# A two-layer MetaFormer kernel on one core: the pipeline one group deeper, the weight broadcast in pieces, the expert sums on VectorE

## The reference

```python
x = x + L0_conv(ln_c(x))      # projection, a linear state per image (KV = B^T V dA, y = C KV + D V), layer norm, W_out
t = t + L0_ffn(ln_t(t))       # mixture of 8 experts, hidden 128, top 2 of a softmax; weights w
x = x + L1_conv(ln_c(x))      # divisive normalisation: x * rsqrt(8x8 channel mix of x^2 + 3x3 depthwise of x^2 + beta)
t = t + L1_ffn(ln_t(t))       # mixture of 8 experts, hidden 256, top 2 of the logits
```

## Time and profile before

| | |
|---|---|
| median of 3 runs (745.37 to 746.63) | 746.52 us |
| the profiled execution's own time | 745.84 us |
| its span in the trace | 744.1 us |
| busy: PE, DVE, ACT, POOL | 566.3, 437.4, 372.7, 245.7 us |
| mean granted TensorE clock | 0.917 of full |

### The profile page before, as it was taken

How to read it: one execution, slowest core, us unless ns; L and a number is a source line. 1 busy time by engine, 2 the same in 40 slices (tenths; PEclk the granted TensorE clock), 3 DMA queues, 4 the chain that set the end, 5 groups by cost and what they waited for, 6 DMA issues and landing times.

```text
span 744.1 us, 10005 instructions
## 1 busy us (share of the span) xinstructions
PE 566.3 (76%) x3778; PEld 276.6 (37%) x3778; DVE 437.4 (59%) x810; ACT 372.7 (50%) x454; POOL 245.7 (33%) x217
## 2 busy tenths in 40 slices
PE   2645675579868995999768986998589968976677
PEld 1242253325423442445224532454244523432333
DVE  3255347454777569574967487756865495546412
ACT  2214322565446655575548554764557564644432
POOL 2020243122523344342442342434434243423103
PEclk9999875799989999899989998999899997989688
DMA  4501400515014500641052401450055005320140
GB/s 66 101 0 43 87 0 0 109 35 104 1 32 98 116 0 15 130 90 27 15 112 52 83 14 49 82 116 1 17 114 114 3 15 115 85 46 0 25 91 28
DMA packets 27838, 41.47 MB, mean 56 GB/s; under 512 B 11792, under 2 KB 19088, under 8 KB 27792
## 3 DMA queue, kind: packets, MB, share of 16 engines
q1 hardware_dynamic: 27152, 38.75, 25.4%
q0 software_dynamic: 640, 2.10, 0.9%
HBM read 38.22 MB, written 2.62 MB: 55 GB/s over the span
## 4 chain that ended last, share of the span: by engine, by line
PE 40%; DVE 27%; ACT 11%; DMA 8%; issue 7%; POOL 6%; SPq 1%; POOLq 0%; DVEq 0%; ACTq 0%
PE yP L863 11%; PE hP L847 11%; DMA WB<-w_scratch 6%; DVE nacc L1149 4%; PE sA L773 3%; PE sA L786 3%; PE sA L780 2%; PE sC L876 2%; ACT H L690 2%; ACT L574 2%; POOL stat_b L494 2%; DVE xsplit L979 2%; DVE xnrm L976 2%; DVE xcen_b L976 2%; PE sA L759 2%
## 5 line engine op out<-in xcount | busy, mean ns | idle before, releaser
L690 ACT ACTIVATE H<-hP,b 128x1024 f32<-128x1024 f32 x192 | 211.0, 1113 | 111.1 <-PE hP L847 108.4
L863 PE MATMUL yP<-H,w 128*64 128x512 f32 x768 | 208.9, 626 | 21.9 <-DVE ACC L1193 14.3
L847 PE MATMUL hP<-xT,w 128*64 128x512 f16 x1536 | 215.7, 406 | 10.6 <-ACT H L690 10.5
L552 POOL TENSOR_TENSOR ACC<-ACC,YW 128x512 f32<-128x512 f32 x96 | 125.4, 1310 | 212.6 <-DVE YW L1193 212.5
L847 PEld LDWEIGHTS hP<-xT,w 128*64 128x64 f16 x1536 | 83.2, 115 | 139.0 <-issue 74.1
L1193 DVE SCALAR_TENSOR_TENSOR YW<-yP,b,WB 128x512 f32<-128x512 f32 x96 | 71.4, 744 | 30.2 <-PE yP L863 30.1
L863 PEld LDWEIGHTS yP<-H,w 128*64 128x64 f32 x768 | 54.1, 143 | 61.7 <-issue 30.6
L1149 DVE SCALAR_TENSOR_TENSOR nacc<-PAD,taps,nacc 128x528 f32<-128x528 f32 x56 | 52.7, 941 | 1.7
L1193 DVE SCALAR_TENSOR_TENSOR ACC<-yP,b,WB 128x512 f32<-128x512 f32 x32 | 23.1, 745 | 41.7 <-DMA WB<-w_scratch 41.7
L1207 DVE TENSOR_TENSOR X<-sC,X 128x256 f32<-128x256 f32 x32 | 13.5, 423 | 53.9 <-PE sC L876 53.9
L876 PEld LDWEIGHTS sC<-fold,ACC 128*128 128x128 f32 x256 | 32.4, 198 | 25.6 <-issue 19.1
(11 more groups left out here) (144 smaller groups left out, 728.4 us busy)
## 6 DMA issues: line engine op xcount, KB each, us to landing
WB<-w_scratch SPq DMA_DIRECT2D x32, 1024.0 KB, 10.1
X<-in_x SPq DMA_DIRECT2D x8, 256.0 KB, 12.0
out<-X POOLq DMA_DIRECT2D x8, 256.0 KB, 2.8
H<-in_L_ffn_W SPq DMA_DIRECT2D x2, 512.0 KB, 6.7
H<-in_L_ffn_W SPq DMA_DIRECT2D x2, 256.0 KB, 4.2
w<-in_L_ffn_W SPq DMA_DIRECT2D x1, 512.0 KB, 5.2
w_scratch<-wTs SPq DMA_DIRECT2D x16, 32.0 KB, 1.8
w<-in_L_ffn_W SPq DMA_DIRECT2D x1, 256.0 KB, 4.4
```

The costliest lines, as they stand in the source:

```text
L552: pool.tensor_tensor(ACC[l][:, cols], ACC[l][:, cols], YW[:, u % 4, :], ALU.add).then_inc(summed, 1)
L690: nc.scalar.activation(H[:, s % RING, :], hP[s % 2][:, :], ACT.Gelu, bias=b1[l][:, e * ch + c:e * ch + c + 1], scale=1.0 / WS)\
L847: mm = nc.tensor.matmul(hP[s % 2][b * C:(b + 1) * C, hf * HALF:(hf + 1) * HALF], w1[l][:, sp, w, b * C:(b + 1) * C], xT[l][g % 2][:, hf * ...
L863: mm = nc.tensor.matmul(yP[hf][a * C:(a + 1) * C, :], w2[l][:, (2 * j + a) * ch + c, :], H[:, (2 * ch * j + 2 * c + a) % RING, hf * HALF:( ...
```

## The change

Four things change.

- **Depth.** A constant DEPTH = 2 enters `moe_start`: moe(0, g) starts at 24(g-2), moe(1, g) stays at 24g+8 as long as a group is still two ahead, and the last two, moe(1, 6) and moe(1, 7), follow each other without a gap (at 144 and 160). A section now holds moe(0, g+2), moe(1, g), most of ab(g+3), and cd(g+1). One section more (moe(0, 1) with ab(2) and cd(0), no moe(1, .)) stands ahead of the first full one, and one full one less follows. X3 gets a third buffer, and ACC is assigned by a table (moe(1, 6) uses the layer-0 accumulator).
- **Places.** cd(g) starts at moe_start(0, g)+16, and its steps are spread: in a section, the nine taps stand on slots 23, 0, 1 and 2 instead of 19 to 21, turn_u on 5 and 6 instead of 0, norm d on 10 instead of 4, its gate on 14 to 17 instead of 6 to 9. The table of ab is the same.
- **Pieces.** WB is filled by four pieces (an expert pair each, two DMAs of 256 KB), each with a semaphore of its own. A piece waits only until that pair of the group before is used. In layer 1 the pieces stand on slots 18, 22, 2 and 6.
- **Sums.** The adds to ACC are made by VectorE right behind the unit, waiting for it; GpSimd makes none.

```diff
 def moe_start(layer, g):
-    return SLOTS * (g - 1) if layer == 0 else SLOTS * g + E
+    if layer == 0:
+        return SLOTS * (g - DEPTH)
+    if g + DEPTH < GROUPS:
+        return SLOTS * g + E
+    return moe_start(1, g - 1) + E * CHUNKS[1]
...
 def cd_start(g):
-    return moe_start(0, g) + E * CHUNKS[0] + LAG + 2
+    return moe_start(0, g) + E * CHUNKS[0] + LAG + 4
...
-    cd=dict(centre_c=1, sums_c=1, norm_c=3, pool0=5, pool1=6, pool2=7, pool3=7, turn_u=10, centre_d=10,
-            sums_d=12, norm_d=14, top2=17, weights=18),
+    cd=dict(centre_c=0, sums_c=1, norm_c=3, pool0=7, pool1=8, pool2=9, pool3=10, turn_u=14, centre_d=15,
+            sums_d=16, norm_d=18, top2=23, weights=24),
...
+            def spread_piece(l, g, j):
                 if g >= 1:
-                    sp.wait_ge(scaled, 8 * (POS[(l, g - 1)] + 1))
+                    sp.wait_ge(scaled, 8 * POS[(l, g - 1)] + 2 * j + 2)
                 for a in range(2):
-                    src = scratch[l][i].rearrange("(j a) n -> a j n", a=2)[a]
-                    sp.dma_start(WB[l][a * C:a * C + C, :, :], src.partition_broadcast(C)).then_inc(w_in[l][i], 16)
+                    sp.dma_start(WB[l][a * C:a * C + C, j, :],
+                                 scratch[l][g % 2][2 * j + a:2 * j + a + 1, :].partition_broadcast(C)
+                                 .rearrange("c a n -> c (a n)")).then_inc(w_in[l][j], 16)
...
-                    pool.tensor_tensor(ACC[l][:, cols], ACC[l][:, cols], YW[:, u % 4, :], ALU.add).then_inc(summed, 1)
...
                     v.scalar_tensor_tensor(out=dst, in0=yP[hf][:, :], scalar=b2[l][:, j:j + 1],
                                            in1=WB[l][:, j, cols], op0=ALU.add, op1=ALU.mult).then_inc(scaled, 1)
+                    if j >= 1:
+                        acc = ACC[ACC_OF[m]][:, cols]
+                        dve.wait_ge(scaled, u + 1)
+                        v.tensor_tensor(acc, acc, dst, ALU.add).then_inc(summed, 1)
```

More of the change, by code:

```diff
@@ L54 @@
 LAG = 4
+DEPTH = 2
 NO_FINAL = (-1, -1, -1, -1)
@@ L58 @@
             mix_out=29, turn_b=32, gate=35, send=36),
-    cd=dict(turn_c=4, pool0=4, turn_u=11, turn_d=15, gate=16, send=19),
-    final=(12, 14, 24, 26))
+    cd=dict(turn_c=5, pool0=6, turn_u=13, turn_d=20, gate=22, send=25),
+    final=(13, 16, 24, 26))
 ACT_AT = dict(
@@ L77 @@
     ab=dict(decay=22, send=35),
-    cd=dict(send=21),
+    cd=dict(send=26, piece1=30, piece2=34, piece3=38),
     final=NO_FINAL)
@@ L136, in build_metaformer @@
         n += E * CHUNKS[m[0]]
+    ACC_OF = {m: 0 if m[0] == 0 or GROUPS - m[1] in range(2, DEPTH + 1) else 1 for m in ORDER}
+    ACC_BEFORE = {}
+    for i in range(2):
+        users = [m for m in ORDER if ACC_OF[m] == i]
+        ACC_BEFORE.update(zip(users[1:], users))
     with ExitStack() as ctx:
@@ L193, in build_metaformer @@
         X2b = sb("X2b", [P, T, C])
-        X3 = [sb(f"X3_{i}", [P, T, C]) for i in range(2)]
+        X3 = [sb(f"X3_{i}", [P, T, C]) for i in range(3)]
         X4 = [sb(f"X4_{i}", [P, T, C]) for i in range(2)]
@@ L281, in build_metaformer @@
         w_out = [[sem(f"w_out{l}_{i}") for i in range(2)] for l in range(2)]
-        w_in = [[sem(f"w_in{l}_{i}") for i in range(2)] for l in range(2)]
+        w_in = [[sem(f"w_in{l}_{j}") for j in range(PAIRS)] for l in range(2)]
         x2b = count("x2b", 1)
@@ L457, in ab @@
                     spread_weights(0, g)
+                    for j in range(PAIRS):
+                        spread_piece(0, g, j)
             def cd(g, k):
@@ L461, in cd @@
                     spread_weights(1, g)
+                    spread_piece(1, g, 0)
+                elif k in ("piece1", "piece2", "piece3"):
+                    spread_piece(1, g, int(k[-1]))
             def moe(m, s):
@@ L541, in moe @@
             def moe(m, s):
[L543 to L551, removed]
-                    pool.tensor_tensor(ACC[l][:, cols], ACC[l][:, cols], YW[:, u % 4, :], ALU.add).then_inc(summed, 1)
+                pass
             def final(m, half):
@@ L1182, in moe @@
                     dve.wait_ge(y_ready, u + 1)
-                    if j == 0 and hf == 0:
-                        dve.wait_ge(w_in[l][g % 2], 32 * (g // 2 + 1))
+                    if hf == 0:
+                        dve.wait_ge(w_in[l][j], 32 * (g + 1))
                     if j == 0:
-                        dst = ACC[l][:, cols]
-                        if g >= 1:
-                            dve.wait_ge(ftr, 2 * POS[(l, g - 1)] + hf + 1)
+                        dst = ACC[ACC_OF[m]][:, cols]
+                        if m in ACC_BEFORE:
+                            dve.wait_ge(ftr, 2 * POS[ACC_BEFORE[m]] + hf + 1)
                     else:
                         dst = YW[:, u % 4, :]
-                        if u >= 4:
-                            dve.wait_ge(summed, sums_until(u - 4))
                     v.scalar_tensor_tensor(out=dst, in0=yP[hf][:, :], scalar=b2[l][:, j:j + 1],
                                            in1=WB[l][:, j, cols], op0=ALU.add, op1=ALU.mult).then_inc(scaled, 1)
+                    if j >= 1:
+                        acc = ACC[ACC_OF[m]][:, cols]
+                        dve.wait_ge(scaled, u + 1)
+                        v.tensor_tensor(acc, acc, dst, ALU.add).then_inc(summed, 1)
             def final(m, half):
@@ L1206, in final @@
                 t4 = slice(4 * half, 4 * half + 4)
-                v.tensor_tensor(dst[g % 2][:, t4, :], ps, res[g % 2][:, t4, :], ALU.add).then_inc(fin, 1)
+                v.tensor_tensor(dst[g % 2][:, t4, :], ps, res[g % len(res)][:, t4, :], ALU.add).then_inc(fin, 1)
             walk(moe, final, ab, cd, DVE_AT)
```

16 lines of the change are left out of this document (8 added, 8 removed).

## The result

The changed kernel took a median of 751.15 us (750.68 to 756.93, 4 runs) beside 745.94 us of the kernel before on the same chip (4 runs). The ratio is 1.0109, with a 95% interval of 1.006 to 1.0159. It is slower by 1.1%, little but clear of noise, since the interval leaves 1 out; the forecast was 714. The profiled execution took 750.79 us, its span is 749.0, and its mean granted TensorE clock is 0.873 (0.917 before).

A forecast was written before the change was run, and what follows sets the result against it. No engine bounds the whole; time is lost in TensorE's waits in full sections and at the ends. Filling 67.4 + first 60.6 + inserted 65 + five full 382 + tail 136 = 711.0 us, plus 2.4: 714 us, range 696 to 736.

The forecast's parts named there:

- with 66.1 busy a full section is 78: Full section: TensorE's 66.1 us busy plus 12.2 of waits, against 80.3 before; bounds 74 and 82.
- a forecast of 12.2: TensorE's waits in a full section: wgt 2.8, turn_u 1.6, Vs 3.1, norm b 4, small 0.7 us; 13.6 before.
- First section, pieces: Start: piece 0 there some 5 us after issue, at 75 rather than 82.5; first section 60.6 us, before 68.6.
- The rival with the fixed parts one after the other: Broadcast: eight DMAs pay their fixed part in turn, 2 us each, 16 us more; about 745 us; chance 0.03.
- Inserted section: Added section with ab(2), moe(0, 1) and the rest of cd(0): 65 us, bounds 60.6 and 73.
- Sums: VectorE's 12 adds per section: +8.8 us, fewer GpSimd hold-ups -6 to -7, net 2; possibly up to 4 more.
- 0.69 nearly everywhere: Sign of being right: VectorE's L976, 1.75 us beside a GpSimd add, takes 0.69 us nearly everywhere.
- Depth: Six full sections of 479 us become five and the cheap inserted one, 447 us: -32; tail +7.
- Tail: From moe(0, 7) on, with 16 slots more: 136 us, bounds 130 and 146; 129.1 before.
- Sums of the rivals: More won: full sections of 75 us give 698, with low ends of tail and start 692; chance 0.15.
- Table loads: Sign of being right, on ScalarE: 26 or more before Exp and Ln, where there are 22.
- The rival of VectorE's order: Full section becomes VectorE's chain, late units delaying yP; 753 us at 86 us a section; chance 0.07.

The follow-up runs named there:

- the filled kernel: Changed kernel plus unread TensorE products ahead of four waits (norm b's transposes 20, state 12, weights' transpose 10, turn_u 7): 704.61 us, ratio 0.9472.

## Why the prediction was wrong

**The step that failed** is "with 66.1 busy a full section is 78". It took TensorE's work as a constant and added the waits. The waits came out at 12.6 for a forecast of 12.2, one by one 2.69 (2.8), 1.90 (1.6), 2.99 (3.1) and 4.87 (4). The work became 72.7: five stretches at half clock per section where one had been. Section by section the filled kernel gives this back: 4.1 us in the inserted one, 4.4, 6.8, 7.1, 8.9 and 8.9 in the full ones, 4.6 in the tail (differences of the sections of the two kernels), 45 of span in all with the first. In a full one the 49 unread products take 11.3 us (1.69, 2.76, 4.49 and 2.33), which leaves 74.87 - 11.3 = 63.6 of TensorE's own work where the changed kernel has 72.7; and 66.1, before, had 2.5 of half clock in it already. The rows held a warning: the earlier trace rows show 0.70 in the first section, where TensorE waits often, and 0.96 in the full ones. I used that only for the ends and the inserted section. A rule I did not weigh stands in the Trainium skill (TensorE: Matmul & The Clock Gate, "HAM oscillation — how this bites in real kernels"): a kernel that waits between bursts of matmuls starts each burst cold. The windows at 479.70 and 516.00, with 0.57 each, agree with it; the one at 500.30, behind no wait, does not come under it.

**Point by point.**
- *First section, pieces*: right. The first unit of moe(0, 0) started at 75.62 (75.5 said), 4.9 us after the first DMA was issued at 70.69; the section was 60.4 (60.6). The rival with the fixed parts one after the other did not happen:

```profile
75.62 0.75 DVE L1200 SCALAR_TENSOR_TENSOR ACC<-yP,b,WB 128x512 f32<-128x512 f32 x1 [8.29 <-DMA WB<-w_scratch]
```

- *Inserted section*: 68.9 for 65, and 64.8 when filled: clock again.
- *Sums*: the size on VectorE was near (+1.4 for +2), the sign of their worth was not weighed. I priced hold-ups by VectorE's busy time, and two of them stood where TensorE waited: -1.8 us per section. The adds themselves took 0.69 us in the median of 96, the longest 1.35, so the 4 us a section that other GpSimd work might have cost them did not come.
- *One hold-up stayed*: I had said 0.69 nearly everywhere, and norm b's own L985 took 1.74 beside GpSimd's X2b, on the chain of the longest wait. In the kernels with VectorE's sums and the old places it takes 0.69, so here the new places brought X2b beside it, and 1.05 of the 4.87 us are this:

```profile
512.84 1.26 POOL L550 TENSOR_TENSOR X2b<-X,bo_rep 128x512 f32<-128x512 f32 x1
```

```profile
512.90 1.74 DVE L985 TENSOR_TENSOR xcen_b<-xcen_b,stat_b 128x512 f32<-128x512 f32 x1 [1.53 <-POOL stat_b L513]
```

- *Depth*: I gave it the swap of a full section for a cheap one, with the tail +7. The swap is there and the tail gives all of it back, and 5 us on top. My -32 for the full sections was 15 for the swap (80 to 65) and 17 for five shorter ones; the swap is worth 11 (77 to 65.9), and the other five are about as long as the six without the depth (76.4 and 76.7 on average, both with the old places).
- *Tail*: 131.8 for 136, within its bounds.
- *Sums of the rivals*: with the low ends of the start and the tail (4.6 and 6 us), 698 becomes 687, not 692.
- *Table loads*: 28 before Exp and Ln for the 26 or more forecast, 22 before. They lay beside TensorE, as said.
- *The rival of VectorE's order* had the right time (753) for a wrong reason: its chance of 0.07 was not for this mechanism. VectorE is busy 54.4 of 85.3 and TensorE waits 2.9 us in all for its buffers.

**What stays open.** Which waits cost the clock is not settled: those of 1.4 to 1.6 us in the kernel before had no half clock behind them, those of 1.9 us and more in the changed one had, but these also lie in other work. The stretch at 500.31, behind the folds (L885) and 16 products of one column (L789), was never tried by itself. It comes with the new places: in the kernel before, where other products stand ahead of the same 16, all six hP groups behind them in the full sections take 1.05 us. It does not come each time: in the changed kernel it is missing in the first full section (246.89, 1.05), in the filled one it is there in three of five, though the order of the products is the same. On what it hangs there no run shows.

## What to carry to other kernels

A wait of TensorE has two prices, its length and the half-speed work behind it, so splitting one long wait into several middling ones can cost more though the sum stays: add up the work at each place's granted clock, not at the section's old busy time. Where a wait can't go, products that nobody reads fill it for nothing, but only where no transfer is next late; look what that work lay beside. And read more than one section: a stretch that is missing in the one you look at may be there in the next. And run the parts of a change by themselves: here two of four were worth 35 us and the other two took 43.

## What the runs showed of the hardware

- Waits of 1.90, 2.69 and 2.99 us were each followed by a stretch at 1.2 GHz (0.58, 0.54 and 0.57 in the windows at 459.80, 445.90 and 479.70), and in one place so was a stretch of narrow products without any wait (0.59 in the window at 500.30), at a price of 1.6 us where it came and went in one kernel. In the section of the earlier trace rows only the wait of 5.74 has it.
- With products whose results are never read in one wait of each section the clock stayed at 1.00 over 375 us, and that kernel is faster than the one without (692.07 beside 706.05).
- Eight DMAs of 256 KB queued one behind the other had their first pair in use 4.9 us after the issue (70.69 to 75.62), where the two of 1 MB had theirs after 12.8; over the whole kernel VectorE waited 12.1 us for WB in place of 41.7.
- A full-size VectorE operation with both inputs in SBUF took 1.74 to 1.76 us beside a GpSimd one in place of 0.69, in the kernel before, the changed and the filled one and in two more; the 128 units, with one input in PSUM, took 0.74 to 0.75 us in the changed kernel.
